# Attention block on one core: q and k stacked per head in DRAM, the turn through three PSUM banks, head sums moved to the last stage

## The reference, cut to what matters

```python
# x (2, 2048, 512), 16 heads of 32, timestep (2,), bias (2, 16, 2048, 2048), mask of padded keys
emb = silu(_sin_emb(timestep)) @ W_ada + b_ada
scale, shift = split(emb[:, None, :], 2)
x = _ln(src) * (1.0 + scale) + shift
q, k, v = heads(x @ Wq + bq), heads(x @ Wk + bk), heads(x @ Wv + bv)
scores = einsum('bhqd,bhkd->bhqk', q / sqrt(32), k) + attention_bias
scores = where(src_mask, -inf, scores)
ctx = einsum('bhqk,bhkd->bhqd', softmax(scores), v)
x = x + (ctx @ Wo + bo)
h = _ln(x) * g2 + beta2
x = x + _gelu2(h @ W1 + b1) @ W2 + b2          # W1 (512, 2048)
out = rotate pairs of x by theta and phi       # x0*ct + x1*st, -x0*st + x1*ct, ...
```

## Time and profile before

| | us |
|---|---|
| median of 3 runs (3857.75 to 3860.23) | 3858.18 |
| profiled execution, whole time | 3858.61 |
| its span, first to last instruction | 3857.0 |
| TensorE busy (matmul) | 3589.8 (93%) |
| VectorE busy | 2561.2 (66%) |
| GpSimd busy | 2165.7 (56%) |
| ScalarE busy | 1899.6 (49%) |

### The profile page before, as it was taken

The page is one execution under the profiler, slowest core; times in us unless marked ns, Lnnn a source line. Parts: engine busy times, 40 slices in busy tenths (PEclk is TensorE's granted clock), DMA queues, the critical chain, the costliest instruction groups (busy, mean ns, idle before and its releaser), DMA issues. The chain is left out here.

```text
span 3857.0 us, 64984 instructions
## 1 busy us (share of the span) xinstructions
PE 3589.8 (93%) x18848; PEld 2074.9 (54%) x18848; DVE 2561.2 (66%) x4882; ACT 1899.6 (49%) x2483; POOL 2165.7 (56%) x595
## 2 busy tenths in 40 slices
PE   6778769999999999999999999999699999999997
PEld 2334336666666666666666666666344444444443
DVE  3444449999989999899999899999322323232232
ACT  1221227777777777777777777777211111111110
POOL 0000059999989999999999999999000000000000
PEclk8889879999999999999999999999799999999999
DMA  5556489999999999999999999997511101101000
GB/s 188 169 173 201 147 288 319 315 313 312 319 348 317 316 312 312 337 331 313 317 315 313 341 319 314 317 313 271 155 22 33 22 11 33 22 22 22 11 11 11
DMA packets 327444, 822.20 MB, mean 213 GB/s; under 512 B 165376, under 2 KB 181760, under 8 KB 250624
## 3 DMA queue, kind: packets, MB, share of 16 engines
q1 hardware_dynamic: 277376, 746.44, 57.6%
q10 hardware_dynamic: 45312, 58.74, 5.6%
q0 software_dynamic: 4736, 16.78, 1.2%
HBM read 737.95 MB, written 83.89 MB: 213 GB/s over the span
## 5 line engine op out<-in xcount | busy, mean ns | idle before, releaser
L450 POOL TENSOR_TENSOR ring<-ring,penb 128x2048 f32<-128x2048 f32 x512 | 2089.4, 4119 | 599.6 <-DMA penb<-pen_scratch 542.5
L555 ACT ACTIVATE ring<-ring,neg_max 128x2048 f32<-128x2048 f32 x512 | 1029.1, 2010 | 515.4 <-DVE neg_max L520 515.4
L618 PEld LDWEIGHTS b_T<-ident,ring 128*128 128x128 f32 x8192 | 886.7, 141 | 623.5 <-ACT probT L564 427.6
L618 PE MATMUL b_T<-ident,ring 128*128 128x128 f32 x8192 | 1158.7, 281 | 1.9 <-DVE probT L492 1.3
L492 DVE COPY probT<-b_T 128x512 f32<-128x512 f32 x1024 | 668.0, 684 | 70.5 <-PE b_T L618 70.5
L506 DVE CUSTOM_DVE_ANT_0 ring<-scores,ring,max_part 128x1024 f32<-128x1024 f32 x512 | 657.6, 1284 | 74.2
L506 DVE CUSTOM_DVE_ANT_0 ring<-scores,ring 128x1024 f32<-128x1024 f32 x512 | 622.2, 1215 | 43.6 <-PE scores L601 43.6
L601 PE MATMUL scores<-keys,queries 128*128 (+1 forms) x2048 | 606.5, 418 | 46.6 <-DMA queries<-q_parts 45.4
L781 POOL TENSOR_TENSOR y_out<-rot_a,rot_b 128x512 f32<-128x512 f32 x32 | 50.3, 1572 | 1020.8 <-DVE rot_b L890 1020.0
L564 ACT COPY probT<-b_T 128x512 f32<-128x512 f32 x1024 | 542.8, 580 | 30.2 <-PE b_T L618 24.0
L634 PE MATMUL bank_ctx<-probT,values 128*32 128x512 f32 x4096 | 546.8, 607 | 0.0
(11 more groups left out here) (91 smaller groups left out, 1926.1 us busy)
## 6 DMA issues: line engine op xcount, KB each, us to landing
ring<-in_fside_Bx16xSxS SPq DMA_DIRECT2D x512, 1024.0 KB, 5.8
keys<-k_parts SPq DMA_DIRECT2D x256, 256.0 KB, 6.8
values<-v_heads ACTq DMA_DIRECT2D x128, 256.0 KB, 6.0
queries<-q_parts SPq DMA_DIRECT2D x512, 64.0 KB, 6.8
pen_scratch<-pen SPq DMA_DIRECT2D x8, 2048.0 KB, 7.2
penb<-pen_scratch SPq DMA_DIRECT2D x32, 512.0 KB, 12.3
xin<-in_x ACTq DMA_DIRECT2D x8, 1024.0 KB, 5.2
mask_in<-in_mask_Bx1xSxS_bk ACTq DMA_DIRECT2D x8, 1024.0 KB, 7.3
```

What stands on the lines that cost most here:

```text
L450: nc.gpsimd.tensor_tensor(ring[:, j, :], ring[:, j, :], penb[:, j, :], ALU.add).then_inc(masked, 1)
L555: nc.scalar.activation(ring[:, k, :], ring[:, k, :], ACT.Exp, bias=neg_max[:, k:k + 1], accum_out=sums[:, k:k + 1]).then_inc(exp_done, 1)
L618: last = nc.tensor.transpose(bankT[n % 2][:, c * P:(c + 1) * P], ring[:, slot, at:at + P], ident[:])
```

## The change

**phase_a.** The columns of Wk and Wq and their biases are put in the order (dimension, head) within a group of four heads: two ScalarE copies, one small matmul. Parts are stored in stacked order, four transfers a group instead of two, to k_rows and q_rows. The loads of x and mask for the first block stand at the very start, and for the next block behind the penalty copies.

**phase_b.** Keys and queries come in one transfer each, with a stride of four rows; the queries are asked for at tiles 0 and 4. VectorE's add writes the negated score and keeps the minimum, which serves exp as its bias directly; neg_max, reciprocal and division are gone. Quarter 3 is copied a step later, between the two adds. The turn uses three banks, and TensorE's waits stand one matmul or two transposes earlier. The close is gone: ctxp is stored as it is, 256 KB a unit; the row sums and minima stay in SBUF. GpSimd's add of the penalty is the same instruction in both.

**phase_c.** The four partial sums of each head are loaded and added (GpSimd; for half of the first block VectorE), the reciprocal sums are spread by ScalarE, turned by TensorE and multiplied in by VectorE in front steps 1 to 4. The rotation of a block is done one tile a step beside the next block (`late`). W1 and W2 are loaded from ScalarE's queue, behind the first part loads.

```diff
-                            to = k_parts if g < DB else q_parts
-                            for n, part in enumerate((part_hi, part_lo)):
-                                sp.dma_start(to[bass.ds(b * 2 + n, 1), i * P:(i + 1) * P, bass.ds(s * TOK, TOK)].rearrange("o r n -> (o r) n"),
+                            to = k_rows if g < DB else q_rows
+                            parts = (part_hi, part_lo, part_lo, part_hi) if g < DB else (part_hi, part_lo, part_hi, part_lo)
+                            for n, part in enumerate(parts):
+                                sp.dma_start(to[bass.ds(b * DB + i, 1), n * P:(n + 1) * P, bass.ds(s * TOK, TOK)].rearrange("o r n -> (o r) n"),
                                              part[:, i, :].bitcast(F32)).then_inc(stored[i], 16)
...
+            def load_tile(u):
+                act.dma_start(xin[:].rearrange("p t n -> p t n"),
+                              x[bass.ds(u, 1)].rearrange("u (t p) n -> p (u t) n", p=P)).then_inc(x_in, 16)
+                act.dma_start(mask_in[:], mask[bass.ds(u, 1)].rearrange("u (t p) n -> p (u t) n", p=P)).then_inc(mask_ld, 16)
...
+            act.wait_ge(w_in, 48)
+            for w, loaded in ((wk, v_out), (wq, xm)):
+                nc.scalar.copy(w[:].rearrange("p c (i d h) -> p (c i) d h", d=DH, h=4),
+                               loaded[:].rearrange("p c (i h d) -> p (c i) d h", d=DH, h=4)).then_inc(by_dim_ready, 1)
...
+                if not (isinstance(u, int) and u == NU - 1):
+                    act.wait_ge(x_used, u + 1)
+                    load_tile(u + 1)
...
+        bankT = [ctx.enter_context(nc.psum_tensor(f"b_T{i}", [P, N], F32)) for i in range(3)]
...
+        def turn_bank(t, n):
+            return bankT[(0, 1, 2, 0)[n] if t % 2 == 0 else (2, 1, 0, 2)[n]]
...
+            def of_head(rows, b, h):
+                group, member = b * DB + h // 4, h % 4
+                return rows[bass.ds(group, 1)].rearrange("o (r m) n -> (o m) r n", m=4)[bass.ds(member, 1)].rearrange("o r n -> (o r) n")
...
-                        for n, part in enumerate((0, 1, 1, 0)):
-                            sp.dma_start(keys[DH * n:DH * (n + 1), bass.ds(it % 2, 1), :].rearrange("p o n -> p (o n)").bitcast(F32),
-                                         k_parts[bass.ds(b * 2 + part, 1), bass.ds(h * DH, DH), :].rearrange("o d n -> (o d) n")).then_inc(k_in, 16)
-                    if qt == 2:
+                        sp.dma_start(keys[:, bass.ds(it % 2, 1), :].rearrange("p o n -> p (o n)").bitcast(F32),
+                                     of_head(k_rows, b, h)).then_inc(k_in, 16)
+                    if qt == 0:
                         sp.wait_ge(scored, it * R * CH + (R + QT * (1 + hh)) * CH)
-                        for n, part in enumerate((0, 1, 0, 1)):
-                            sp.dma_start(queries[DH * n:DH * (n + 1), hh, :].bitcast(F32),
-                                         q_parts[bass.ds(b * 2 + part, 1), bass.ds(h * DH, DH), bass.ds((pair * 2 + hh) * TOK, TOK)].rearrange("o d n -> (o d) n")).then_inc(q_in[hh], 16)
+                        sp.dma_start(queries[:, hh, :].bitcast(F32),
+                                     of_head(q_rows, b, h)[:, bass.ds((pair * 2 + hh) * TOK, TOK)]).then_inc(q_in[hh], 16)
...
-                                                   scalar=max_part[:, j, c - 1:c] if c else MASKED,
-                                                   op0=ALU.add, op1=ALU.max,
-                                                   accum_out=max_part[:, j, c:c + 1]).then_inc(added, 1)
+                    nc.vector.tensor_tensor_reduce(out=at, in0=scores[c][:], in1=at, scale=-1.0,
+                                                   scalar=low_part[:, j:j + 1] if c else -MASKED,
+                                                   op0=ALU.add, op1=ALU.min,
...
-                if live(i, NT):
-                    dve.wait_ge(added, i * CH + CH)
-                    nc.vector.tensor_scalar(neg_max[:, j:j + 1], max_part[:, j, CH - 1:CH], -2.0, 0.5, ALU.mult, ALU.mult).then_inc(max_ready, 1)
-                copy_quarter(it, j, 2)
-                if dividing:
-                    dve.wait_ge(exp_done, i - 1)
-                    nc.vector.reciprocal(recip[:, hh, :], sums[:, hh * QT:(hh + 1) * QT]).then_inc(recip_ready, 1)
-                copy_quarter(it, j, 3)
...
                 add(it, j, 0)
+                copy_quarter(it, j, 3, 3)
                 add(it, j, 1)
+                copy_quarter(it, j, 2, 2)
...
-                    act.wait_ge(max_ready, i)
-                    nc.scalar.activation(ring[:, k, :], ring[:, k, :], ACT.Exp, bias=neg_max[:, k:k + 1],
-                                         accum_out=sums[:, k:k + 1]).then_inc(exp_done, 1)
+                    k, trip = (j - 1) % R, it if j else it - 1
+                    act.wait_ge(added, i * CH)
+                    if j == 0:
+                        nc.scalar.copy(low_all[:, bass.ds(trip, 1), :].rearrange("p o n -> p (o n)"), low[:]).then_inc(low_kept, 1)
+                    nc.scalar.activation(ring[:, k, :], ring[:, k, :], ACT.Exp, bias=low[:, k:k + 1], scale=-1.0,
+                                         accum_out=column(sums_all, trip, k)).then_inc(exp_done, 1)
...
+                unit, hh = closing(it, j), 0 if j < QT else 1
+                if j % QT == 1 and live(unit, UNITS):
+                    act.wait_ge(pv_done, PV0 + unit + 1)
+                    act.wait_ge(ctx_stored, unit * 16 + 16)
+                    nc.scalar.copy(ctxp[:], bank_ctx[:]).then_inc(ctx_copied, 1)
+                    if not known(it) or it < TRIPS:
+                        load_values(it, hh)
+                if j % QT == 2 and live(unit, UNITS):
+                    trip = it - 1
+                    act.wait_ge(ctx_copied, unit + 1)
+                    act.dma_start(ctx_scratch[bass.ds((trip // H) * 2 * H + hh * H + trip % H, 1)].rearrange("o p n -> (o p) n"),
+                                  ctxp[:]).then_inc(ctx_stored, 16)
...
+            def free_before_turn(it, j, c):
+                t = it * R + j - 2
+                if live(t, NT):
+                    if c == 0:
+                        pe.wait_ge(exp_done, t + 1)
+                    else:
+                        need(pe, out_dve, t * 2 - 1)
...
+                if n == 2 and live(t, NT):
+                    need(pe, out_dve, t * 2)
+                for c in range(QR):
+                    if c == 2:
+                        if n == 0 and live(t, NT):
+                            need(pe, out_act, t * 2)
+                        if n == 1:
+                            copied_before_weigh(it, j)
+                        if n == 2 and live(t, NT):
+                            pe.wait_ge(out_act, t * 2 + 1)
+                    if live(t, NT):
+                        at = (QR * n + c) * P
+                        last = nc.tensor.transpose(turn_bank(slot, n)[:, c * P:(c + 1) * P], ring[:, slot, at:at + P], ident[:])
...
-            def close(it, j):
-                unit = closing(it, j)
-                if live(unit, UNITS):
-                    pe.wait_ge(ctx_copied, unit + 1)
-                    pe.wait_ge(ctx_normed, unit + 1)
-                    for t in range(QT):
-                        last = nc.tensor.matmul(bank_sum[:, t * DH:(t + 1) * DH], ctxp[:, t * P:(t + 1) * P], sel4[:],
-                                                start=True, stop=True)
-                    last.then_inc(ctx_summed, 1)
...
+            for f in range(FB + 2):
+                ffn(0, f)
+                front(1, f)
+            with eng.Fori(1, NU - 1) as u:
                 for f in range(FB + 2):
                     ffn(u, f)
-                    if f < FB:
-                        front(u + 1, f)
+                    front(u + 1, f)
+                    late(u - 1, f)
             for f in range(FB + 2):
                 ffn(NU - 1, f)
+                late(NU - 2, f)
+            for t in range(QT):
+                late(NU - 1, t)
...
+                for c in range(DB):
+                    if isinstance(v, int) and c == 2:
+                        load_vectors()
+                    need(sp, ctxT_ready, v * DB + c - 1)
+                    for k in range(4):
+                        sp.dma_start(parts[DH * k:DH * (k + 1), c % 2, :, :],
+                                     ctx_scratch[bass.ds(v * H + 4 * c + k, 1)].rearrange("o (g d) q -> d (o g) q", d=DH)).then_inc(part_ld[c % 2], 16)
                 need(sp, x2_ready, v * QT)
...
+            def add_parts(v, c):
+                pool.wait_ge(part_ld[c % 2], v * 128 + (c // 2) * 64 + 64)
+                nc.gpsimd.tensor_tensor(parts[:, c % 2, 0:2, :], parts[:, c % 2, 0:2, :], parts[:, c % 2, 2:4, :], ALU.add).then_inc(halved, 1)
+                pool.wait_ge(halved, added_by_pool(v, c))
+                nc.gpsimd.tensor_tensor(parts[:, c % 2, 0, :], parts[:, c % 2, 0, :], parts[:, c % 2, 1, :], ALU.add).then_inc(summed, 1)
...
+            def between(v):
```

(24 more changed lines are left out.)

384 lines of the change are left out of this document (190 added, 194 removed).

## The result

| | before | after |
|---|---|---|
| median of the runs | 3858.9 us (4 runs, 3857.8 to 3860.2) | 3742.6 us (4 runs, 3741.7 to 3745.5) |
| profiled execution, its span | 3858.6, 3857.0 us | 3742.7, 3741.0 us |
| granted clock over the span | 0.965 | 0.972 |

The ratio is 0.970, 95% interval 0.9683 to 0.9717: 116 us less, where 112 were forecast. The predicted 3746 us was 3.4 us too high. The terms behind it were less exact than their sum.

What follows compares the result with a forecast made beforehand. Attention was taken as paced by VectorE and TensorE together, 4% above GpSimd's floor, the last stage by TensorE. Terms -4 - 62 - 9 - 37 = -112 took the 3857.0 us span to 3745, forecast 3746 us; 8 in 10: 3722 to 3793.

Steps and rivals of the forecast that it cites:

- VectorE and TensorE set the pace together, 4% above GpSimd's floor: Attention before the change: the tile takes 4.2 us, set by VectorE and TensorE, against GpSimd's 4.08.
- All consumers come under 4.08 and GpSimd becomes the pace: Attention after the change: the other engines need under 4.08 us a tile, GpSimd sets the pace; -62 us.
- where I left 21: Attention: GpSimd's idle time between first and last add falls from 83.3 to 21 us, giving -62 us.
- Its step lies between 3.4 and 3.8 us: Attention: TensorE's time per tile after the close goes, a third bank is added and waits are moved.
- The trip's single key transfer and the queries save issues on SP, not bytes: Attention loads: one transfer in place of several saves only issues on the SP queue; no gain in bytes.
- The rival with nearly full queues: Attention: DMA limited to 342 GB/s, late loads at new mask groups cost about +25, 3771 us; chance 0.16.
- The rival with rows 32 KB apart: Attention: strided q and k rows, or a limit already reached, hold queues at 315 GB/s; +127, 3873 us; chance 0.06.
- The dearer add: Attention: VectorE's negating add costs +0.25 us each, so attention keeps its pace; about 3850 us; chance 0.04.
- at about 30 us: +8: Last stage's opening: first output-projection matmul at about 30 us into the stage, before 22.4; +8, bounds +3 and +15.
- -45 net: Last stage: spreading the rotation removes 40.7 us of waits and 15 of slow restarts, a new wait adds 11.
- The new wait for the widened reciprocal: Last stage, step 1 of a block: TensorE waits 1.6 us for ScalarE's wide reciprocal, seven times; +11 us.
- -4: Projections: the sum of its terms, with first x and mask loads no longer waiting for start-up arithmetic; -4 us.

## Why the prediction was right, and where it was not

*"VectorE and TensorE set the pace together, 4% above GpSimd's floor"*: that it was not GpSimd is shown by the kernel before with half the mask (no change). That it was TensorE's order with its waits for the copies is read from the waits. The change took away the close, neg_max and the division, added a bank and moved waits, all at once; which of these took the tile under 4.08 us was not tried one by one, but for the order of VectorE's copies, which was not needed. *"All consumers come under 4.08 and GpSimd becomes the pace"*: right, shown from both sides, by that run's 0 and by the 88 us of the same edit after the change. GpSimd's idle time fell to 3.4 us where I left 21. The later mask groups cost nothing: 418 GB/s stood in the window where I saw 373, and no ring or mask tile came late. That is 18 of the 19 us that this term was short.

*"Its step lies between 3.4 and 3.8 us"* for TensorE: too low. It is 3.90, seen only once GpSimd was out of the way. The 3.4 us counted work alone and left out that TensorE's weight loads still wait 0.8 us a tile for VectorE's copy. The mistake had no effect on the time, but the margin under GpSimd was 0.18 us and not 0.3 to 0.7.

*"The trip's single key transfer and the queries save issues on SP, not bytes"*: the step that failed, though the sum came out. No bytes, indeed, but queue time: 3.77 us a tile against 4.19. I costed the layout at nothing, and without it the change would have been a loss (3910 us). I had only looked at GB/s, for which 416 in a window promised room; here the queues took longer for the same bytes in another form. The sum was right because both edits came together. In the kernel before the layout alone is worth 26 us; of the 81 us from first to last add 24 are then stalls at the start and at the mask groups that go with it, and the other 57 are the pace: 2148.4 / 512 = 4.20 us a tile against 2091.8 / 512 = 4.09.

The rival with nearly full queues was wrong for this kernel, with 337 GB/s carried at 0.93 and 353 at 0.97. Its 342 GB/s came from 315 divided by 0.92, where the row has 0.93 and full queues read 1.02. Its idea, that the margin is small, was right. The rival with rows 32 KB apart named the wrong half of the layout: stacked rows in one transfer are part of the window at 416 GB/s (525 to 545 us, where a head's keys and queries were issued), and neighbouring rows in four are slow. The dearer add did not come (1.23 and 1.28 us).

Opening of the last stage, *"at about 30 us: +8"*: mis-sized, and outside its bounds of +3 and +15; it was at 52.7, +29.5 to the first up product. I saw the shared queues, but not that ScalarE itself issues the weights ahead of its first copy, and that four issues which took 4.55 us take 11.38 with four more transfers of 1 MB on the way. Taking them away gave 22 back, and with them gone the first output product starts at 30.5 us, the place that was forecast.

*"-45 net"* in the steady last stage: -49.8, right by its mechanism. The lower clock of the slow groups, which the earlier trace rows do not show, is in the trace: a mean of 0.56 from 3053.8 to 3060.3 us and 0.72 from 3189.8 to 3194.9, and 1.00 from 3200 to 3203.6. The new wait for the widened reciprocal is 1.4 us, as worked out (1.6); the run with the rotation in one piece gives 57 for it, since that wait then takes the old one's place.

Start, *"-4"*: -2.7 at GpSimd's first add, a small miss. VectorE's small loads came 3.9 us later behind x and mask. Putting these behind brought 2 us at the first k product and nothing behind the stage.

That the time came within 3.4 us is in part luck: attention gave 22 us more than forecast with its tail, the steady last stage 5, and the opening of that stage took 21.5 of it back.

## What to carry to other kernels

Before an edit is called free, put every shared resource beside the new pace in us per tile, the DMA queues by their busy share and not by GB/s: a layout that was worth 26 us at 4.20 us a tile was worth 168 us at 4.08. Such a share is read late in a stage: with short transfers from stacked rows GpSimd ran 128 tiles without a wait before the shortage showed. Halving one engine's work in both kernels (leaving part of the result out) is the cheapest proof of who sets the pace, and tells what the next bound is. In a stage's opening, look at what stands in the same engine's instruction order as its first dependent operation, transfers' issues included.
